# Three of 34 passes of a fused attention kernel written out, and 16 products put before one wait

## The chip, the cores and the metric

The kernel runs on one core of a Trainium2 chip. What counts is the time of one execution on the device in microseconds; of several executions the median is given. The engines are TensorE (PE in the profile, its weight loads PEld), VectorE (DVE), ScalarE (ACT), GpSimd (POOL) and SyncE (SP), which here only starts transfers.

## What is computed

A batch of 64 sequences of 128 rows with 320 channels, with a context of 128 x 192 each, goes through two blocks. All values are float32.

```python
# first block, 8 heads
hs = mha(x @ Wq, enc @ Wk, enc @ Wv)                   # FIRST: enc = the context's first 124 rows
ca_hs1 = mha(ca_q1, x, x)                              # CA: ca_q1 from the context's last 4 rows, "the tokens"
ca_hs2 = mha(ca_hs1 @ Wq, ca @ Wk_ca, ca @ Wv_ca)      # over 4 keys
x = (hs + ca_hs2) @ Wout + b_out + x
# second block, 20 heads
h1 = ln(x); x = attn(h1, h1, q1, k1, v1, o1_w) + x     # SELF
h2 = ln(x); x = attn(h2, context, q2, k2, v2, o2_w) + x  # CROSS
h3 = ln(x); a, g = split(h3 @ ff_w1 + ff_b1)
x = (a * gelu(g)) @ ff_w2 + ff_b2 + x
```

## The kernel before

The batch is cut into 32 steps of two sequences (G = 2, STEPS = 32), and the work on a step into three stages that run in three passes: the first block of step i, the two attentions of the second block of step i - 1, and the feed-forward part (ff) of step i - 2. One pass of the loop does the first stage of one step, the second of the one before and the third of the one before that, so that each engine always has work of another step beside a wait. The loop runs 33 passes, i = 0 to 32, and a tail does the last feed-forward. In pass 0 there is no step for the attentions of the second block nor for ff, in pass 1 none for ff, in pass 32 none for the first block; the loop does those blocks all the same, on zeros or stale tiles, and nothing reads what they give. Before the loop a head loads and scales the weights.

Everything is written out by hand per engine: five instruction streams, each with a loop of its own over i, which meet through semaphores. The list BODY names the results that TensorE puts into its six PSUM banks in turn ("jobs"). `j_next` waits until the bank's last reader is done, and each job ends with an increment of `j_full`, which a reader on ACT (`a_done`) or DVE (`v_done`) waits for. All waits are on counts that grow by a fixed amount per pass (`done`), so each pass must raise each semaphore by the same number.

Names that matter here:

- Heads are taken in units of four. Unit n has the scores (`scores(i, n)`, job S*n*), the row maxima (`maxima`, L1104, on DVE), the maxima turned (`turn_maxima`, L1609, job mx*g*), the scores again with the maximum subtracted (`exponents`, job T*n*), the exponential on ACT (`exps`, L810 and L811), its low part on POOL (`low_probabilities`, L540) and the product with the values (`attend`). Units 0 to 3 are CA, 4 to 13 SELF, 14 to 23 CROSS, 24 to 27 FIRST.
- All matmuls go through `mm` (L1487).
- The query and key tiles of an attention are put together ("stacked") by transfers that SP starts (`spread`, L406): three chunks by three parts for each of Q0T and K0T (tiles Q0s, K0s), K1T (Ks), Q1T and Q2T (Qs). K1T and Q1T (`chunk16`) are split by DVE (`whole_shifted`, L1005) and POOL (`low_split`, L547) first. The cross keys go through DRAM (L394, L398). SP does all in the fixed order of `one_pass`: Q0T, K1T, Q1T, the table M (L439), ten loads of the next step (L384 to L391; `load_next` first waits for DVE's `vca`, the values of the tokens, L1195), K0T 0 and 1, the cross keys, Q2T, K0T 2, K2T, two stores.
- `scores(i, 4)`, the first of SELF, waits for the first chunk of K1T and of Q1T. This wait is called **the S4 wait** below. Ahead of it on TensorE stand the feed-forward jobs ff2 and ff3; behind it S4, S5, T2, vca, S6, S7, V1_0, T3, attends 0 and 1, S8, S9 and mx2.
- DVE takes the extremes of the next step's x (`extremes_x`, L1030, tile xin) for a scale; TensorE turns them (`extremes_turned`, L1716, job mT) and spreads them (mB), and the scale goes over DVE and ACT to POOL.
- The last blocks of a pass are the projections, residuals (L1166) and norms (L1177), with a small power on POOL between (L597, L598). The norm of the first block is what K1T and Q1T of the next pass are made from. DVE's part of Q0T (`low_chunk`, L1011) stands behind that norm in DVE's order.

```python
def one_pass(i, stores):
    put_low(i, "Q0T", 0, Q0s, cQ, Q_PARTS)
    ...
    load_products(i)
    load_next(i)
```

Of the kernel before, what the change touches and what calls it, by code (L numbers as in the profile page):

```python
# [7 lines left out]
B, S, H, C = 64, 128, 320, 192  # L8
# [184 lines left out]
def build(nc, d, out):  # L193
# [4 lines left out]
    with ctx:  # L198
# [182 lines left out]
        def _(sp):  # L381
# [66 lines left out]

            def one_pass(i, stores):
                put_low(i, "Q0T", 0, Q0s, cQ, Q_PARTS)  # L450
                put_low(i, "Q0T", 1, Q0s, cQ, Q_PARTS)
                put_low(i, "Q0T", 2, Q0s, cQ, Q_PARTS)
                put_split(i, "K1T", 0, Ks, cK, K_PARTS)
                put_split(i, "K1T", 1, Ks, cK, K_PARTS)
                put_split(i, "K1T", 2, Ks, cK, K_PARTS)
                put_split(i, "Q1T", 0, Qs, cQ, Q_PARTS)
                put_split(i, "Q1T", 1, Qs, cQ, Q_PARTS)
                put_split(i, "Q1T", 2, Qs, cQ, Q_PARTS)
                load_products(i)
# [12 lines left out]
                put_out(i, 1, stores)  # L472
# [31 lines left out]
        def _(pool):  # L504
# [45 lines left out]
            def x_values(i, b, rest):  # L550
# [4 lines left out]
                scaled = rest[:, b, :].rearrange("p (h e) -> p h e", h=HEADS0)  # L555
                if not isinstance(i, int):
# [79 lines left out]
            nc.gpsimd.memset(whole[:, :, :], 0.0).then_inc(split_done, SPLITS_STEP)  # L636
            with nc.Fori(0, STEPS + 1, engines=[pool.engine], hint_back_edge=True) as i:
                links[0] = 0
# [54 lines left out]
                token_queries(i)  # L693
                assert links[0] == POOL_LINKS
            last_bias(STEPS + 1)

        @block.scalar
        def _(act):
# [115 lines left out]
            def link(i, ins):  # L814

                links[0] += 1
                ins.then_inc(act_done, 1)
                act.wait_ge(act_done, links[0] if isinstance(i, int) else i * ACT_LINKS + ACT_HEAD_LINKS + links[0])

# [58 lines left out]
            assert links[0] == ACT_HEAD_LINKS  # L878
            with nc.Fori(0, STEPS + 1, engines=[act.engine], hint_back_edge=True) as i:
                L = LOOP_JOBS  # L880
# [91 lines left out]
                assert order.next == PER["A"]  # L972
                assert links[0] == ACT_LINKS
            order.restart()
            for t in range(FFT):
# [3 lines left out]
        def _(dve):  # L979
# [372 lines left out]

            with nc.Fori(0, STEPS + 1, engines=[dve.engine], hint_back_edge=True) as i:
                L = LOOP_JOBS
# [119 lines left out]
                assert order.next == PER["V"]  # L1474
                assert links[0] == STEP_LINKS, links[0]
            order.restart()
            for t in range(FFT):
# [5 lines left out]
        def _(pe):  # L1483
# [313 lines left out]

            with nc.Fori(0, STEPS + 1, engines=[pe.engine], hint_back_edge=True) as i:
                L = LOOP_JOBS
# [161 lines left out]
                out_proj(i, 0, 1)  # L1961
                assert filled[0] == PER["J"]
            filled[0] = 0
            for t in range(FFT):
# [75 lines left out]
```

## Time and profile before

| | |
|---|---|
| median of 3 runs | 3696.13 us (3693.54 to 3698.23) |
| the profiled execution | 3700.3 us |
| its span, first to last instruction | 3698.4 us |
| mean granted TensorE clock | 0.956 of full |
| PE busy | 3427.4 us, 93% |
| ACT, DVE, POOL busy | 67%, 61%, 56% |
| first matmul of the loop | 99.36 us |
| start of the tail's feed-forward | 3665.30 us |
| instructions | 114778 |

The page gives the busy time of each engine over the whole span, the same in 40 slices with the granted clock, and the waits by what ended them. Since the program repeats itself, the trace is best read inside one pass (about 108 us), and by comparing passes. PE counts as busy while a matmul is under way, at either clock, so PE's 93% says little about how fast the work goes.

### The profile page before, as it was taken

What the parts mean: (1) busy time and instruction counts of PE and PEld (TensorE: products, weight loads), DVE (VectorE), ACT (ScalarE), POOL (GpSimd) and SP (SyncE); (2) the same over time, 40 slices, a digit from 0 to 9 for tenths busy, and PEclk for the clock granted to TensorE, in tenths of its full rate; (3) what the DMA queues carried; (4) which work ended last, traced back from release to release, by engine and by line L of the source; (5) the groups of instructions that cost most, each with busy time, mean ns of one, the idle gap of its engine ahead of it and who ended that gap; (6) DMA issues with size and microseconds to landing.
All of it is one profiled execution on the core that took longest, in us unless ns stands there. A gap on an engine that the chain in (4) does not pass through costs nothing.

```text
span 3698.4 us, 114778 instructions
## 1 busy us (share of the span) xinstructions
PE 3427.4 (93%) x38842; PEld 2788.6 (75%) x38842; DVE 2269.9 (61%) x5540; ACT 2494.6 (67%) x4428; POOL 2070.6 (56%) x2307
## 2 busy tenths in 40 slices
PE   7899999999999999999999999999999999999999
PEld 7677787777777777777777777787777777777777
DVE  6566666566566656666655666665566666556665
ACT  3576676767767676776767677676767767676774
POOL 1565555556655555655555566555556655555664
PEclk6899999999999999999999999999999999999999
DMA  5211111221111122111112211111221111112111
GB/s 185 56 42 44 40 43 48 50 53 46 47 44 42 45 50 52 46 47 42 43 46 50 52 46 47 42 43 46 50 52 46 47 42 43 45 50 52 46 47 26
DMA packets 316267, 183.06 MB, mean 49 GB/s; under 512 B 50107, under 2 KB 315379, under 8 KB 315507
## 3 DMA queue, kind: packets, MB, share of 16 engines
q1 hardware_dynamic: 303936, 173.93, 18.5%
q8 instruction: 367, 6.01, 0.7%
q10 hardware_dynamic: 11955, 3.04, 0.4%
q14 instruction: 9, 0.07, 0.0%
HBM read 70.59 MB, written 24.67 MB: 26 GB/s over the span
## 4 chain that ended last, share of the span: by engine, by line
PE 44%; issue 20%; POOL 11%; DVE 7%; SPq 6%; ACT 5%; DMA 5%; POOLq 1%; ACTq 1%; DVEq 0%
PE bank L1487 41%; SPq L406 5%; DMA Qs<-cQ 5%; DVE mx L1104 4%; PE bank L1514 2%; ACT PT L811 2%; POOL rstd L598 2%; POOL cK L547 1%; POOL cQ L547 1%; ACT L794 1%; POOL c L592 1%; ACT P L810 1%; POOL X L517 1%; POOL rstd L597 1%; PE bank L1609 1%
## 5 line engine op out<-in xcount | busy, mean ns | idle before, releaser
L540 POOL TENSOR_TENSOR PT<-P,PT 128x512 f16<-128x512 f32 (+1 forms) x924 | 1066.9, 1156 | 808.5 <-ACT PT L811 806.2
L1487 PE MATMUL bank<-hT,w_ff_w 128*128 128x256 f16 x5440 | 644.0, 273 | 29.3 <-DVE G L1018 29.3
L1104 DVE TENSOR_REDUCE mx<-bank 128x4 f32<-128x512 f32 (+1 forms) x924 | 588.5, 682 | 115.7 <-PE bank L1487 108.3
L1487 PEld LDWEIGHTS bank<-hT,w_ff_w 128*128 128x128 f16 x5440 | 518.3, 98 | 100.5 <-DVE G L1018 41.0
L1487 PE MATMUL bank<-mxs,pick 84*128 84x128 f16 (+1 forms) x3696 | 513.6, 223 | 0.0
L1183 DVE SCALAR_TENSOR_TENSOR F<-bank,ff_b,gate 128x256 f32<-128x256 f32 x340 | 160.0, 481 | 435.9 <-ACT gate L794 435.9
L1487 PE MATMUL bank<-w_ff,F 128*128 128x320 f32 x1360 | 418.4, 443 | 1.3 <-DVE F L1183 1.3
L1487 PEld LDWEIGHTS bank<-mxs,pick 84*128 84x128 f16 (+1 forms) x3696 | 380.6, 105 | 4.0
L1487 PE MATMUL bank<-Ks,Qs 96*128 96x128 f16 x2640 | 236.0, 235 | 148.3 <-DMA Qs<-cQ 144.3
L1487 PEld LDWEIGHTS bank<-V,PT 128*128 128x128 f16 (+1 forms) x9504 | 336.2, 96 | 48.7 <-issue 23.5
L1487 PE MATMUL bank<-Qs,Ks 96*128 96x128 f16 x2640 | 359.3, 219 | 11.2 <-DVE mxs L1113 7.3
L1487 PE MATMUL bank<-V,PT 128*128 128x17 f16 (+1 forms) x9504 | 352.2, 172 | 0.0
L1487 PEld LDWEIGHTS bank<-Ks,Qs 96*128 96x128 f16 x2640 | 175.4, 105 | 219.3 <-issue 188.1
L794 ACT ACTIVATE gate<-bank,ff_b,scale 128x256 f32<-128x256 f32 x340 | 184.0, 562 | 211.1 <-PE bank L1487 172.7
L810 ACT ACTIVATE P<-bank,log_p,held 128x512 f32<-128x512 f32 x330 | 253.6, 768 | 78.8 <-PE bank L1487 44.4
L597 POOL TENSOR_TENSOR rstd<-mv,eps 128x1 f32<-128x1 f32 x198 | 44.7, 226 | 467.5 <-DVE mv L1171 467.5
L1487 PEld LDWEIGHTS bank<-w_ff,F 128*128 128x128 f32 x1360 | 239.9, 190 | 78.9 <-issue 6.5
L1487 PEld LDWEIGHTS bank<-Qs,Ks 96*128 96x128 f16 x2640 | 252.1, 98 | 30.3 <-DVE mxs L1113 22.7
L810 ACT ACTIVATE P<-bank,log_p,exp_self 128x512 f32<-128x512 f32 x330 | 254.8, 772 | 19.6 <-POOL PT L540 9.8
L811 ACT ACTIVATE PT<-bank,log_p,exp_self 128x512 f16<-128x512 f32 x330 | 253.8, 769 | 0.0
L811 ACT ACTIVATE PT<-bank,log_p,held 128x512 f16<-128x512 f32 x330 | 252.3, 765 | 0.0
L1005 DVE TENSOR_SCALAR whole<-bank,q_factor,qk_b 128x256 f32<-128x256 f32 (+1 forms) x297 | 157.4, 539 | 124.8 <-ACT cQ L723 89.7
(290 smaller groups left out, 7310.6 us busy)
## 6 DMA issues: line engine op xcount, KB each, us to landing
Qs<-cQ SPq DMA_DIRECT2D x402, 64.0 KB, 2.6
Ks<-scratch_k SPq DMA_DIRECT2D x99, 160.0 KB, 4.6
Ks<-cK SPq DMA_DIRECT2D x198, 64.0 KB, 2.6
Q0s<-cQ SPq DMA_DIRECT2D x198, 60.0 KB
K0s<-cK SPq DMA_DIRECT2D x198, 60.0 KB
xin<-in_x SPq DMA_DIRECT2D x34, 320.0 KB, 3.5
out<-X SPq DMA_DIRECT2D x64, 160.0 KB, 1.8
xT<-in_xT SPq DMA_DIRECT2D x68, 128.0 KB, 2.1
```

Of the source, the lines that this page charges most:

```text
L406: sp.dma_start(dst[y * e:(y + 1) * e, at:at + heads, :], src[0:rows[k], part, k, :])\
L540: nc.gpsimd.tensor_tensor(PT[0:keys, n % PT_SLOTS, 1, :], P[0:keys, n % P_SLOTS, :], PT[0:keys, n % PT_SLOTS, 0, :], ALU.subtract).then_in ...
L547: nc.gpsimd.tensor_tensor(dst[0:r, 1, k, :], whole[0:r, m % 3, :], dst[0:r, 0, k, :], ALU.subtract)\
L597: link(i, nc.gpsimd.tensor_tensor(rstd[:, j, b:b + 1], mv[:, j, b, 1:2], eps[:, :], ALU.add))
L598: nc.gpsimd.tensor_tensor(rstd[:, j, b:b + 1], rstd[:, j, b:b + 1], minus_half[:, :], ALU.pow)\
L794: nc.scalar.activation(gate[:, t % 2, :], bank[:, 0:GS], ACT.Gelu, scale=scale[:, 1:2], bias=ff_b[:, FFT + t:FFT + t + 1]).then_inc(a_done, 1)
L810: nc.scalar.activation(P[0:keys, n % P_SLOTS, :], bank[0:keys, :], ACT.Exp, bias=log_p[0:keys, :], scale=by)
L811: nc.scalar.activation(PT[0:keys, n % PT_SLOTS, 0, :], bank[0:keys, :], ACT.Exp, bias=log_p[0:keys, :], scale=by).then_inc(a_done, 1)
L1005: nc.vector.tensor_scalar(whole[0:r, m % 3, :], bank[0:r, 0:GS], q_factor[0:r, :], qk_b[0:r, c + k:c + k + 1], ALU.mult, ALU.add).then_inc ...
L1104: nc.vector.tensor_reduce(mx[:, g % 2, 4 * u:4 * u + 4], bank[:, :].rearrange("p (h s) -> p h s", h=4)[:, :, 0:keys], axis=AX.X, op=ALU.ma ...
L1183: nc.vector.scalar_tensor_tensor(out=F[:, t, :], in0=bank[:, GS:2 * GS], scalar=ff_b[:, t:t + 1], in1=gate[:, t % 2, :], op0=ALU.add, op1= ...
L1487: return nc.tensor.matmul(o, lhsT, rhs, start=start, stop=stop)
```

## The change

There are two parts.

**Written out.** Passes 0, 1 and 32 leave the loop, on all five engines, and are written out in straight code without the blocks that have no step: pass 0 without SELF, CROSS and ff; pass 1 without ff; pass 32 without CA, FIRST and what they need. The loop runs i = 2 to 31. Where blocks are left out, a `left_out` raises the semaphores by what they would have: on ACT, DVE and POOL by a drain with an increment, on TensorE by one product of 1 x 1 for each semaphore, behind the wait for the bank of the next job. On SP passes 0 and 1 were written out already; of the transfers only the table M and the ten loads of pass 32 go, the other transfers of passes 0, 1 and 32 stay, those of blocks without a step too.

**16 products.** In `scores`, `j_next` moves ahead of the waits for the stacked tiles, and at S4 16 matmuls of 128 x 128 weights by 512 columns (f16, from the ff weights) go into S4's bank between the two. S4 writes over them; nothing reads them. They stand in passes 1 to 32.

```diff
@@ -94,6 +94,7 @@
 SPLITS_STEP = 9
 LOADS_STEP = 16 * 10
 STACK_LOADS = 16 * 3
+KEEP_BUSY = 16
...
-            def one_pass(i, stores):
+            def one_pass(i, stores, last=False):
...
-                load_products(i)
-                load_next(i)
+                if not last:
+                    load_products(i)
+                    load_next(i)
...
-            with sp.Fori(2, STEPS + 1) as i:
+            with sp.Fori(2, STEPS) as i:
                 one_pass(i, True)
+            one_pass(STEPS, True, True)
+            for landed in stacked["K0T"]:
+                sp.wait_ge(landed, (STEPS + 1) * 48)
...
+            def left_out(i, split_done_by=0, low_p_by=0, pool_done_by=0, rstd_ready_by=0, xc_ready_by=0, c16_ready_by=0, xa_ready_by=0, vx_ready_by=0, x16_ready_by=0, ca_ready_by=0):
+
+                if split_done_by:
+                    pool.drain().then_inc(split_done, split_done_by)
+                if low_p_by:
+                    pool.drain().then_inc(low_p, low_p_by)
...
-            with nc.Fori(0, STEPS + 1, engines=[act.engine], hint_back_edge=True) as i:
+            def left_out(i, a_done_by=0, c_scaled_by=0, c_high_by=0, act_done_by=0, next_ready_by=0, x_scaled_by=0, x_high_by=0, exp4_ready_by=0, factor_ready_by=0):
+
+                if a_done_by:
+                    act.drain().then_inc(a_done, a_done_by)
...
-                elif b == 0 and att != CA:
+                bank = j_next(i, LOOP_JOBS, f"S{n}")
+                if (att, b, u) == (SELF, 0, 0):
+
+                    for _ in range(KEEP_BUSY):
+                        mm(bank[:, 0:2 * GS], w16["ff_w1"][:, 0, 0, 0:128], w16["ff_w1"][:, 0, 0, 0:2 * GS])
+                if b == 0 and att != CA:
...
-                bank = j_next(i, LOOP_JOBS, f"S{n}")
...
-            with nc.Fori(0, STEPS + 1, engines=[pe.engine], hint_back_edge=True) as i:
+            def left_out(i, j_full_by=0, pv_done_by=0):
+
+                n = min(filled[0], PER["J"] - 1)
+                bank_free(i, LOOP_JOBS, n)
+                o = j_bank[n % J_BANKS][0:1, 0:1]
+                if pv_done_by:
+                    mm(o, one_row[:, 0:1], one_row[:, 0:1]).then_inc(pv_done, pv_done_by)
+                if j_full_by:
+                    mm(o, one_row[:, 0:1], one_row[:, 0:1]).then_inc(j_full, j_full_by)
+                filled[0] += j_full_by
+
+            i = 0
+            L = LOOP_JOBS
+            filled[0] = 0
+            left_out(i, j_full_by=1)
+            chunk(i, "Q0T", 0, "Wq", x16, PASSES_X, AT0, CH0)
+            chunk(i, "Q0T", 1, "Wq", x16, PASSES_X, AT0, CH0)
+            left_out(i, j_full_by=1)
+            chunk(i, "Q0T", 2, "Wq", x16, PASSES_X, AT0, CH0)
...
+            extremes_turned(i, L)
+            left_out(i, pv_done_by=2, j_full_by=5)
+            extremes_everywhere(i, L, 2)
+            left_out(i, pv_done_by=6, j_full_by=6)
+            chunk(i, "K0T", 1, "Wk", c16, PASSES_C, AT0, CH0)
+            left_out(i, j_full_by=3)
+            scores4(i)
+            left_out(i, j_full_by=6)
+            chunk(i, "K0T", 2, "Wk", c16, PASSES_C, AT0, CH0)
+            left_out(i, j_full_by=6)
+            values(i, "V0", 1, "Wv")
+            chunk(i, "K2T", 0, "k2", c16, PASSES_C, AT1, CH1)
+            left_out(i, j_full_by=7)
...
+            with nc.Fori(2, STEPS, engines=[pe.engine], hint_back_edge=True) as i:
...
```

On TensorE, at the S4 wait in the loop (L1494 and L2233 are `done`, the number for a wait on a bank; L1595 and L2339 the wait for the stacked tiles), before:

```order
L1494 REGISTER_ALU
L1487 MATMUL bank<-hT,w_ff_w 128x256 x16
L1494 REGISTER_ALU
L1487 MATMUL bank<-hT,w_ff_w 128x256 x16
L1595 ISA
L1494 REGISTER_ALU
L1487 MATMUL bank<-Ks,Qs 128x128 x4
```

and now:

```order
L2233 REGISTER_ALU
L2226 MATMUL bank<-hT,w_ff_w 128x256 x16
L2233 REGISTER_ALU
L2226 MATMUL bank<-w_ff_w 128x512 x16
L2339 ISA
L2226 MATMUL bank<-Ks,Qs 128x128 x4
```

Between ff3 and S4 the number for the bank comes before the wait for the transfers, and the 16 products stand between them.

On TensorE, in pass 0, from the turned extremes (ident,ext_wide; mT) over mB (diag,ones_square) and the chunks 1 and 2 of K0T (c,w_Wk) with s4 (M,whole) between, as it is now:

```order
L2459 MATMUL bank<-ident,ext_wide 128x128
L2226 MATMUL bank<-one_row 1x1 x2
L2226 MATMUL bank<-diag,ones_square 128x2
L2226 MATMUL bank<-one_row 1x1 x2
L2226 MATMUL bank<-c,w_Wk 120x256 x5
L2226 MATMUL bank<-one_row 1x1
L2226 MATMUL bank<-M,whole 128x32 x6
L2226 MATMUL bank<-one_row 1x1
L2226 MATMUL bank<-c,w_Wk 80x256 x5
```

Before, the last of these stood behind this much more (from K0T's chunk 1 to chunk 2):

```order
L1487 MATMUL bank<-c,w_Wk 120x256 x5
L1494 REGISTER_ALU
L1487 MATMUL bank<-w_o_w,hTn 128x320 x8
L1494 REGISTER_ALU
L1518 REGISTER_ALU
L1487 MATMUL bank<-w_o_w,hTn 128x320 x8
L1494 REGISTER_ALU
L1487 MATMUL bank<-hT,w_ff_w 128x256 x16
L1494 REGISTER_ALU
L1565 ISA
L1487 MATMUL bank<-M,whole 128x32 x6
L1674 ISA
```

Between the chunks of K0T the projections of SELF and the feed-forward jobs are gone, and a 1 x 1 product stands for them.

## Rows read from the trace of the kernel before

**Rows 1.** Waits of the whole span: who waited, for whom, us in total, times, longest.
```profile
PE bank L1487 <- DMA Qs<-cQ: 144.3, 49, 5.0
...
SPq L444 <- DVE vca L1195: 62.4, 31, 2.4
```

**Rows 2.** Stretches of pass 13, its start and around S4: length, PE, PEld, DVE, ACT, POOL busy, granted clock.
```profile
1508.00:1514.00 6.00, 5.24 (x48) 4.71 (x47) 4.33 (x12) 3.11 (x7) 3.00 (x6) 1.00 0.02 5
1528.50:1533.00 4.50, 0.00 (x0) 0.00 (x0) 0.94 (x2) 1.28 (x3) 3.86 (x5) 0.97 0.30 78
1533.00:1539.50 6.50, 6.35 (x34) 4.00 (x35) 3.06 (x5) 2.73 (x3) 1.15 (x1) 0.50 0.17 46
```

**Rows 3.** Timeline of pass 13: start, us, engine, line, what [idle before, ended by].
```profile
1524.79 3.66 PE L1487 MATMUL bank<-hT,w_ff_w 128*128 128x256 f16 x32
...
1533.15 1.03 PE L1487 MATMUL bank<-Ks,Qs 96*128 96x128 f16 x8 [4.71 <-DMA Qs<-cQ]
...
1537.40 0.48 DVE L1195 TENSOR_TENSOR vca<-bank,maskv 64x320 f32<-64x320 f32 x1 [2.32 <-PE bank L1487]
...
1541.88 0.28 PE L1609 MATMUL bank<-ident,mx 128*20 128x128 f32 x1 [0.26 <-DVE mx L1104]
...
1547.49 0.82 DVE L1030 TENSOR_REDUCE ext_wide<-xin 128x1 f32<-128x640 f32 x1 [0.24 <-DMA xin<-in_x]
```

**Rows 4.** Timeline of pass 5, with the S4 of pass 6.
```profile
671.41 0.62 PE L1487 MATMUL bank<-Ks,Qs 96*128 96x128 f16 x8 [3.92 <-DMA Qs<-cQ]
...
674.70 0.48 DVE L1195 TENSOR_TENSOR vca<-bank,maskv 64x320 f32<-64x320 f32 x1 [1.57 <-PE bank L1487]
...
678.75 0.28 PE L1609 MATMUL bank<-ident,mx 128*20 128x128 f32 x1 [0.26 <-DVE mx L1104]
...
684.32 0.82 DVE L1030 TENSOR_REDUCE ext_wide<-xin 128x1 f32<-128x640 f32 x1 [0.19 <-DMA xin<-in_x]
...
777.30 0.39 PE L1487 MATMUL bank<-Ks,Qs 96*128 96x128 f16 x4 [4.02 <-DMA Qs<-cQ]
```

**Rows 5.** A stretch of pass 5, columns as in rows 2.
```profile
672.40:676.90 4.50, 4.50 (x24) 2.50 (x23) 2.50 (x5) 2.73 (x3) 1.15 (x1) 0.62 0.16 44
```

**Rows 6.** Timeline of pass 14: mx2, and extremes that waited for no transfer.
```profile
1650.11 0.28 PE L1609 MATMUL bank<-ident,mx 128*20 128x128 f32 x1 [0.26 <-DVE mx L1104]
...
1655.40 0.81 DVE L1030 TENSOR_REDUCE ext_wide<-xin 128x1 f32<-128x640 f32 x1
```

**Rows 7.** Timeline of SP's queue, pass 0 and the start of pass 1.
```profile
113.96 7.35 SPq L406 DMA_DIRECT2D Q0s<-cQ  x9
...
127.89 6.41 SPq L406 DMA_DIRECT2D Qs<-cQ  x9
...
142.09 0.45 SPq L391 DMA_DIRECT2D xin<-in_x  x1
...
166.66 1.75 SPq L398 DMA_DIRECT2D Ks<-scratch_k  x3
173.61 5.75 SPq L406 DMA_DIRECT2D Qs<-cQ  x9
179.40 2.45 SPq L406 DMA_DIRECT2D K0s<-cK  x3
...
221.79 7.20 SPq L406 DMA_DIRECT2D Q0s<-cQ  x9
```

**Rows 8.** The page, part 6: a transfer, how often, KB each, us from issue to landing.
```profile
xin<-in_x SPq DMA_DIRECT2D x34, 320.0 KB, 3.5
```

**Rows 9.** Timeline of pass 0: TensorE.
```profile
132.77 0.62 PE L1487 MATMUL bank<-Ks,Qs 96*128 96x128 f16 x8 [2.19 <-DMA Qs<-cQ]
...
178.13 2.37 PE L1487 MATMUL bank<-w_ff,F 128*128 128x320 f32 x8
```

**Rows 10.** Timeline of pass 0: the first exponential of CROSS, the last of the pass.
```profile
184.86 0.78 ACT L810 ACTIVATE P<-bank,log_p,held 128x512 f32<-128x512 f32 x1 [1.34 <-PE bank L1487]
...
206.83 0.80 ACT L811 ACTIVATE PT<-bank,log_p,factor 124x512 f16<-124x512 f32 x1
```

More of the change, by code:

```diff
@@ L638, in _ @@
+            token_queries(i)
+            assert links[0] == POOL_LINKS
+            with nc.Fori(2, STEPS, engines=[pool.engine], hint_back_edge=True) as i:
                 links[0] = 0
@@ new lines, in _ @@
+            high_tokens(i, L)
+            turn_factors(i, done(i, PER["V"] - 1, "V"))
+            assert order.next == PER["A"]
+            assert links[0] == ACT_LINKS
+            i = 1
+            L = LOOP_JOBS
+            order.restart()
+            links[0] = 0
+            left_out(i, a_done_by=1)
+            high_chunk(i, "Q0T", 0, cQ, CH0[0], FQ0)
+            high_chunk(i, "Q0T", 1, cQ, CH0[1], FQ0)
+            high_blocks(i, "XT0_0", hTn, 0)
+            high_chunk(i, "Q0T", 2, cQ, CH0[2], FQ0)
@@ new lines, in _ @@
+            high_out(i, 2, 1)
+            exps(i, 26)
+            exps(i, 27)
+            high_out(i, 0, 0)
+            first_part(i, "V2", 1, V2, HEADS1, D1, fixed[:, F2:F2 + 1])
+            high_out(i, 0, 1)
+            high_blocks(i, "XT2_0", hT3, 0)
+            high_blocks(i, "XT2_1", hT3, 1)
+            high_tokens(i, L)
+            turn_factors(i, done(i, PER["V"] - 1, "V"))
+            assert order.next == PER["A"]
+            assert links[0] == ACT_LINKS
+            with nc.Fori(2, STEPS, engines=[act.engine], hint_back_edge=True) as i:
@@ new lines, in _ @@
+            i = 0
+            L = LOOP_JOBS
+            links[0] = 0
+            order.restart()
+            left_out(i, v_done_by=1)
+            low_chunk(i, "Q0T", 0, cQ, CH0[0], FQ0)
+            low_chunk(i, "Q0T", 1, cQ, CH0[1], FQ0)
+            left_out(i, v_done_by=1)
+            low_chunk(i, "Q0T", 2, cQ, CH0[2], FQ0)
+            left_out(i, v_done_by=4)
+            maxima(i, 0)
+            maxima(i, 1)
+            left_out(i, v_done_by=2)
+            maxima(i, 2)
+            maxima(i, 3)
@@ new lines, in _ @@
+            normalise(i, 7)
+            left_out(i, xh_ready_by=1)
+            whole_heads(i, 1)
+            left_out(i, xh_ready_by=1)
+            low_part(i, "V2", 1, V2, HEADS1, D1, fixed[:, F2:F2 + 1])
+            residual(i, 0, 0)
+            low_out(i, 0, 1)
+            left_out(i, v_done_by=2)
+            low_tokens(i, L)
+            residual(i, 0, 1)
+            norm(i, 0, 0)
+            norm(i, 0, 1)
+            assert order.next == PER["V"]
+            assert links[0] == STEP_LINKS, links[0]
@@ new lines, in _ @@
+            low_maxima(i, 3)
+            copy_hT(i, "caT0", 0, CH0)
+            copy_hT(i, "caT1", 1, CH0)
+            diagonal(i, L, 2)
+            normalise(i, 2)
+            step_sizes(i, L)
+            left_out(i, v_done_by=1)
+            low_out(i, 1, 0)
+            normalise(i, 3)
+            left_out(i, v_done_by=3)
+            low_out(i, 1, 1)
+            low_chunk(i, "K0T", 1, cK, CH0[1], FK0)
+            residual(i, 1, 0)
+            residual(i, 1, 1)
+            norm(i, 1, 0)
@@ new lines, in _ @@
+            norm(i, 1, 1)
+            left_out(i, v_done_by=1)
+            scores4(i)
+            low_blocks(i, "XT1_0", hTn, 0)
+            low_blocks(i, "XT1_1", hTn, 1)
+            left_out(i, v_done_by=1)
+            whole_shifted(i, "Q2T", 0, 6)
+            whole_shifted(i, "Q2T", 1, 6)
+            whole_shifted(i, "Q2T", 2, 6)
+            low_chunk(i, "K0T", 2, cK, CH0[2], FK0)
+            maxima(i, 14)
+            maxima(i, 15)
+            left_out(i, v_done_by=1)
+            maxima(i, 16)
@@ L1354, in _ @@
+            assert order.next == PER["V"]
+            assert links[0] == STEP_LINKS, links[0]
+            with nc.Fori(2, STEPS, engines=[dve.engine], hint_back_edge=True) as i:
                 L = LOOP_JOBS
@@ new lines, in _ @@
+            residual(i, 2, 0)
+            left_out(i, v_done_by=1)
+            residual(i, 2, 1)
+            left_out(i, v_done_by=1, dve_done_by=1, o_done_by=1)
+            norm(i, 2, 0)
+            left_out(i, v_done_by=1)
+            norm(i, 2, 1)
+            left_out(i, v_done_by=3, dve_done_by=1, var_ready_by=1)
+            low_blocks(i, "XT2_0", hT3, 0)
+            low_blocks(i, "XT2_1", hT3, 1)
+            left_out(i, v_done_by=2, dve_done_by=1, var_ready_by=1, xh_ready_by=2)
+            assert order.next == PER["V"]
```

1000 lines of the change are left out of this document (994 added, 6 removed).

## The prediction, written before the changed kernel ran

> **What bounds the kernel now.** I read the waits first, then one pass in stretches and as a timeline, then the passes against each other. The list of waits has TensorE standing still for the transfers of the stacked queries: 144.3 us in 49 times [rows 1]. The long ones are one per pass, at S4, so at most 144.3 / 33 = 4.4 us each. The stretches show what follows: TensorE does nothing for some 4.5 us, at full clock nearly to the end, and the next 6.5 us run at a granted clock of 0.50, the lower of its two levels, 1.2 instead of 2.4 GHz, while it is busy throughout [rows 2]. So the wait costs twice: once as idle time, and once more in the products behind it.
>
> The timeline gives the size. From S4 to mx2, the first thing that waits for the row maxima of SELF, pass 13 takes 1541.88 - 1533.15 = 8.7 us [rows 3]. In pass 5 the clock came back sooner (0.62 over 4.5 us) and the same stretch took 7.3 us [rows 4, 5]. The next S4 then came 105.9 us after this one [rows 4], where the mean of the 31 distances from pass 1 on is 107.8. Three more passes with 7.35 us to mx2 are followed by 106.3, 106.8 and 106.8 us. The trace thus holds the experiment already: what is gained in this stretch is gained in the pass.
>
> What hangs on it is DVE's order. The extremes of xin begin 5.3 us behind mx2 where their transfer is there (1655.40 - 1650.11) [rows 6], otherwise when it lands. Over the 30 passes 2 to 31 they begin on average 14.4 us behind S4 (14.3 in pass 13, 12.9 in pass 5) [rows 3, 4], and from them to the next pass all passes take the same within 0.1 us. I therefore price the change at this point.
>
> **The 16 products.** *Their own cost.* 32 products of 256 columns take 3.66 us to the end of the last, so 0.109 us each [rows 3]; 512 columns twice that, 16 make 3.5 us. They begin when ff3 is issued and S4's bank was read long before, so they lie inside the wait of at most 4.4 us on average, which stays: it ends when transfers land that SP issues back to back from Q0T on (27 of them in 20.3 us in pass 0, 113.96 to 134.30) [rows 7]. Without that cover they would cost their 3.5 us in every pass. Behind TensorE in this time stands nothing but S4.
>
> *The clock.* About 0.9 us of idle time is left, 0.2 to 1.5 over the passes. The trace has two neighbours: 6.00 - 5.24 = 0.8 us without work at the start of each pass leave the clock at 1.00 [rows 2]; idle of 2.2 us before S4 of pass 0 was followed by the low clock [rows 9]. 0.9 is nearer the first, and I take it that the clock stays up in passes 2 to 31.
>
> *What that is worth.* At full clock the stretch is S4 and S5 0.45, T2 0.55, vca 1.2 (4 float32 products at (2.37 - 0.43) / 7 = 0.28, and a gap) [rows 9], S6 and S7 0.45, V1_0 1.1 (8 x 320 columns at 0.136), T3 0.47, attend 0.3, and S8 to mx2 1.2: together 5.7 us, against 8.7. DVE would then ask for xin at 5.7 + 5.3 = 11.0. It isn't there: SP loads it only after vca, which DVE finishes 4.7 us behind S4 in pass 13 and 3.8 in pass 5 [rows 3, 4]. xin could be read 9.6 and 9.1 us after that; with vca done at 2.8 it lands at 11.9 to 12.8, since SP's present wait for vca, 62.4 / 31 = 2.0 us [rows 1], is just used up. I take 12.4. So the extremes move from 14.4 to 12.4, 2.0 us per pass, and the transfer of xin is what comes late next. Over the 30 passes in the loop: **60 us**. Bounds: as good as pass 5 only, 14.4 - 12.9 = 1.5, makes 45; if xin never held, 14.4 - 11.0 = 3.4, makes 102. The page on "TensorE: Matmul & The Clock Gate" of the Trainium skill, in its section on the back-to-back issue gap, gives about 131 ns per product of 512 columns for a sustained stream of load and product; by it, an estimate, the 16 would take 2.1 us and leave 2.2 us idle. No row here has 512 columns in this type; those of 256 scale to 218 ns, and what it would mean if the page were right is a rival below.
>
> In passes 1 and 32 I count nothing for the products: ff2 and ff3, or CA's jobs, no longer stand before the wait, it grows to some 7 to 9 us, and what is left beyond 3.5 is longer than the 2.2 that was enough in pass 0.
>
> **Written out, pass 0.** Of TensorE's work most goes, but the path becomes SP's queue and the chain of four units. Q0T's transfers start at 113.96 as before; they and those of K1T and Q1T are still made, to 134.3 [rows 7]. The loads, which waited for vca, start at once, 2.5 us sooner, xin is issued at 139.6 rather than 142.09 and lands 3.5 us later [rows 7, 8], at 143.1. Two reductions, mT, mB and K0T 1 through ACT and DVE: an estimate of 6 us from the single durations, 149. Then, each by its row: K0T 1 2.45, cross keys 1.75, Q2T 5.75, K0T 2 2.45, at 161.4, and 2.0 to land: 163.4 for FIRST's second unit, where it is 179.40 + 2.45 + 2.0 = 183.9 now [rows 7]. From there to Q0T of pass 1 it is 37.9 us now, with CROSS's ten units between; then it is maxima 4.5, four exponentials of 1.35 and copies 6.7, the last low part 1.2, and the tail of products, residual and norm, for which I take 10 (now 221.79 - 207.63 = 14.2, in a queue with others) [rows 7, 10]: 22.4, so 185.8. **36 us** saved; bounds 28 (twice the tail's slack, and products at the low clock) and 42.
>
> **Pass 1.** It lacks ff: 160 products of 256 columns at 0.109 and 40 in float32 at 0.28, 28 us of TensorE. Up to S4 it was cover for SP's transfers, and gives nothing. Between S4 and the end of SELF ACT's exponentials set the pace. Behind them the gelus and products go out of a serial chain, about 3 us, and two feed-forward pieces before mx4 2 more; from 184.86 on ACT works without a break to 207.63 [rows 10] and is not shortened. **5 us**; bounds 0 and 15.
>
> **Pass 32.** No CA, FIRST or chunks: mx2 needs 5 instead of 8.9 us at the low clock (no T2, vca, T3, attends), some 4; two copies before mx4 1; the last exponentials and the first block's tail leave the end, where the tail's ff waits only for CROSS's norm, 6; one less job at the start 1. **12 us**; bounds 6 and 20.
>
> Drains, 1 x 1 products and longer programs: at most some 0.1 us each on engines that have idle time; they count as nothing as long as the semaphores they raise are not the last ones, and make 5 us at worst in three passes. The loop's exit shows no gap in front of the tail, so I add none.
>
> **The sum.** 60 + 36 + 5 + 12 = 113 us. Against the profiled execution's 3700.3 us (span 3698.4) that is 3587; it lies 4.2 above the median of 3696.13, so the median becomes **3583 us**.
>
> **The rivals.**
> - *The clock still falls.* The rest of the wait, or the mix of work behind it, is enough to lower it. For it: the 2.2 us of pass 0 [rows 9]. Against it: only 0.9 us are left. Only the 53 us of the written-out passes remain: 3643. Chance 0.10. The page's shorter products would lead here too: products in half their time leave 2.2 us, as in pass 0, and the time is the same 3643 us, worked out from the same rows; chance 0.05.
> - *xin does not hold.* The transfer lands sooner than I think, or DVE's delay isn't on TensorE's path, whose jobs behind mT then run on: up to 102 + 53 = 155, 3541. Chance 0.12.
> - *Less from the passes written out.* The chain of four units runs at the low clock and the left-out jobs make waits of their own; half of 53: 3610. Chance 0.08.
> - *Slower.* The products themselves run at 1.2 GHz: 7.0 us, 2.6 beyond the wait, 32 times 83, less 53: 3726. It decides from the point where they end 53 / 32 = 1.7 us behind the landing. Against it: the clock is at 1.00 when the wait begins, and stays for most of it [rows 2]. Chance 0.02.
>
> My forecast has 0.63. **The range**, 3540 to 3620, takes in the forecast with its bounds, the free xin and the smaller gain of the passes, and leaves out the fallen clock and the slower case, 0.17. Below 0.2%, 7.4 us, a measurement of this kernel can't tell from no change; only a cancelling of gain and longer wait would fall there, 0.01. Faster 0.97, slower 0.02.
>
> **What the changed profile would show.** The 16 products right behind ff3, 3.5 us; a wait of about 0.9 us; granted clock 1.00 over passes 2 to 31, mean about 0.99; mx2 5.7 us behind S4; the extremes at about 12.4 with some 1.3 us of wait for xin in every pass; a distance of 105.8 us between S4s; S4 of pass 1 near 204; the tail's ff at 3552. A clock of 0.5 behind S4 in the loop, or extremes that wait for nothing, would show the second term wrong; an S4 of pass 1 beyond 212 the third.

## The result, and the profile after

| | before | changed |
|---|---|---|
| median | 3696.97 us | 3739.02 us |
| range of the runs | 3693.54 to 3698.23 | 3731.01 to 3757.15 |
| profiled execution, its span | 3700.3, 3698.4 | 3757.15, 3755.2 |
| mean granted clock | 0.956 | 0.939 |

The ratio is 1.0124, with a 95% interval of 1.0091 to 1.0157: the changed kernel is **slower by 1.2%**. The forecast was 3583 us, 3.1% faster. The profiled execution of the changed kernel was its slowest of four, 18 us over the median; its shares below add up to its own 3755.2, so they are somewhat larger than those of a middling execution.

I split both traces at S4 of passes 1, 2 and 32 (239.60, 347.41 and 3580.56 before; 206.73, 317.94 and 3632.07 now):

| stretch | before | now | difference | forecast |
|---|---|---|---|---|
| start to S4 of pass 1 | 239.6 | 206.7 | -32.9 | -36 |
| pass 1 | 107.8 | 111.2 | +3.4 | -5 |
| passes 2 to 31, each | 107.77 | 110.47 | +2.7 | -2.0 |
| pass 32 and tail | 117.8 | 123.1 | +5.3 | -12 |

The loop carries the result: 30 x 2.7 = 81 us in this execution. The list of waits of the changed kernel, the whole span, TensorE's and DVE's part (who waited, for whom, us in total, times, longest):

```profile
PE bank L2459 <- DVE V L1443: 65.6, 31, 3.3
PE bank L2226 <- DMA Qs<-cQ: 36.8, 56, 3.0
PE bank L2226 <- issue: 26.0, 10, 3.4
...
DVE ext_wide L1449 <- DMA xin<-in_x: 78.2, 33, 8.7
```

The 144.3 us of [rows 1] have become 36.8. In their place stands a wait at mT (L2459), once per pass, at most 3.3 us: mT's bank and its operand come from DVE, and DVE waits 78.2 us for xin. The main rows of one pass, pass 10, as the timelines of TensorE, DVE and SP's queue have it:

```profile
1191.87 3.62 PE L2226 MATMUL bank<-w_ff_w 128*128 128x512 f16 x16
1196.17 0.61 PE L2226 MATMUL bank<-Ks,Qs 96*128 96x128 f16 x8 [0.68 <-DMA Qs<-cQ]
1201.88 0.28 PE L2352 MATMUL bank<-ident,mx 128*20 128x128 f32 x1 [0.26 <-DVE mx L1523]
1205.63 0.40 SPq L392 DMA_DIRECT2D xin<-in_x  x1
1209.20 0.82 DVE L1449 TENSOR_REDUCE ext_wide<-xin 128x1 f32<-128x640 f32 x1 [1.95 <-DMA xin<-in_x]
1211.14 0.32 PE L2459 MATMUL bank<-ident,ext_wide 128*128 128x128 f32 x1 [1.90 <-DVE V L1443]
1242.75 0.62 PE L2226 MATMUL bank<-Ks,Qs 96*128 96x128 f16 x8
```

Up to mx2 this is the forecast to the tenth: 16 products in 3.6 us, 0.7 us of wait left, mx2 5.71 us behind S4 (8.7 in [rows 3]). Then TensorE stands 1.9 us at mT, and from mT to S14 (the last row) it takes 31.6 us; before it was 28.7 on average. The stretches of the same pass say why (columns as in rows 2: length, the five engines, granted clock, and then the DMA engines' share and GB/s):

```profile
1191.50:1196.00 4.50, 3.99 (x21) 1.78 (x19) 0.94 (x2) 1.88 (x3) 4.46 (x6) 1.00 0.31 80
1196.00:1202.00 6.00, 5.58 (x78) 4.27 (x79) 4.33 (x8) 4.13 (x6) 1.16 (x1) 1.00 0.26 67
1209.00:1212.00 3.00, 1.10 (x25) 0.93 (x23) 2.74 (x7) 2.03 (x4) 2.19 (x3) 1.00 0.08 21
1212.00:1220.00 8.00, 8.00 (x94) 7.00 (x91) 1.83 (x8) 4.34 (x6) 3.72 (x4) 0.57 0.01 2
```

The clock is 1.00 behind S4, where it was 0.50, and 0.57 behind mT, where it was 1.00. **The low clock has moved with the wait.** It follows mT in 27 of the 30 passes of the loop. In 8 of the 30 there is a second stop at the end of the pass, before ff0, the first products of the next one, and nothing in the profile ends it. The timeline of TensorE at the start of pass 16, and the stretch behind it, where the clock is down too (0.61):

```profile
1832.61 2.44 PE L2226 MATMUL bank<-hT,w_ff_w 128*128 128x256 f16 x16 [2.63 <-issue]
```

```profile
1833.00:1837.00 4.00, 4.00 (x25) 3.66 (x24) 0.72 (x1) 1.84 (x3) 3.77 (x5) 0.61 0.00 0
```

So theory A: the forecast holds up to mx2, the wait for xin becomes idle time of TensorE, and this idle time costs the clock. Its rival, B: it is the written-out code that slows the loop.

### The profile page after: what moved, and what is told of

Same layout as the page of the kernel before. It is cut to its first block, busy times and chain, and to the rows that moved or that the text cites. A ratio compares the mean times of both kernels' runs of the same rounds, so it can differ in the third digit from the quotient of the medians.

```text
span 3755.2 us, 111650 instructions
## 1 busy us (share of the span) xinstructions
PE 3464.1 (92%) x38162; PEld 2789.7 (74%) x38162; DVE 2197.6 (59%) x5366; ACT 2419.3 (64%) x4281; POOL 2012.4 (54%) x2242
## 3 DMA queue, kind: packets, MB, share of 16 engines
q8 instruction: 353, 5.78, 0.6%
## 4 chain that ended last, share of the span: by engine, by line
PE 46%; issue 15%; SPq 9%; DVE 8%; POOL 8%; DMA 7%; ACT 5%; POOLq 1%; ACTq 1%; DVEq 1%
PE bank L2226 43%; SPq L407 5%; DMA Qs<-cQ 4%; DVE mx L1523 3%; DMA xin<-in_x 3%; PE bank L2253 2%; SPq L386 1%; POOL cQ L552 1%; ACT PT L977 1%; ACT P L976 1%; SPq L385 1%; POOL rstd L603 1%; DVE V L1443 1%; POOL cK L552 1%; ACT L960 1%
## 5 line engine op out<-in xcount | busy, mean ns | idle before, releaser
L545 POOL TENSOR_TENSOR PT<-P,PT 128x512 f16<-128x512 f32 (+1 forms) x896 | 1034.0, 1156 | 879.1 <-ACT PT L977 864.6
L1523 DVE TENSOR_REDUCE mx<-bank 128x4 f32<-128x512 f32 (+1 forms) x896 | 571.1, 681 | 107.2 <-PE bank L2226 101.9
L2226 PE MATMUL bank<-mxs,pick 84*128 84x128 f16 (+1 forms) x3584 | 535.3, 233 | 0.0
L2226 PE MATMUL bank<-Qs,Ks 96*128 96x128 f16 x2560 | 393.6, 237 | 20.0 <-DVE mxs L1532 14.4
L2226 PE MATMUL bank<-w_ff,F 128*128 128x320 f32 x1280 | 396.3, 445 | 1.3 <-DVE F L1602 1.3
L960 ACT ACTIVATE gate<-bank,ff_b,scale 128x256 f32<-128x256 f32 x320 | 173.6, 563 | 206.1 <-PE bank L2226 171.1
L2226 PEld LDWEIGHTS bank<-Qs,Ks 96*128 96x128 f16 x2560 | 267.4, 107 | 38.6 <-DVE mxs L1532 29.1
L2226 PEld LDWEIGHTS bank<-w_ff,F 128*128 128x128 f32 x1280 | 227.2, 191 | 75.4 <-issue 7.7
L2226 PE MATMUL bank<-Ks,Qs 96*128 96x128 f16 x2560 | 209.8, 221 | 48.0 <-DMA Qs<-cQ 36.8
L2226 PEld LDWEIGHTS bank<-Ks,Qs 96*128 96x128 f16 x2560 | 158.0, 98 | 105.6 <-issue 37.7
```

The costliest lines, as they stand in the source:

```text
L545: nc.gpsimd.tensor_tensor(PT[0:keys, n % PT_SLOTS, 1, :], P[0:keys, n % P_SLOTS, :], PT[0:keys, n % PT_SLOTS, 0, :], ALU.subtract).then_in ...
L960: nc.scalar.activation(gate[:, t % 2, :], bank[:, 0:GS], ACT.Gelu, scale=scale[:, 1:2], bias=ff_b[:, FFT + t:FFT + t + 1]).then_inc(a_done, 1)
L1523: nc.vector.tensor_reduce(mx[:, g % 2, 4 * u:4 * u + 4], bank[:, :].rearrange("p (h s) -> p h s", h=4)[:, :, 0:keys], axis=AX.X, op=ALU.ma ...
L2226: return nc.tensor.matmul(o, lhsT, rhs, start=start, stop=stop)
```

## The experiments

### Each part alone

The first kernel is the one before with only this edit in `scores`; the second is the changed kernel without the products.

```diff
+                bank = j_next(i, LOOP_JOBS, f"S{n}")
+                if (att, b, u) == (SELF, 0, 0):
+                    for _ in range(KEEP_BUSY):
+                        mm(bank[:, 0:2 * GS], w16["ff_w1"][:, 0, 0, 0:128], w16["ff_w1"][:, 0, 0, 0:2 * GS])
```

> The kernel before, all 33 passes in the loop, with only the 16 products. Theory A (the wait has moved: SELF is quicker up to mx2, then mT stands 2.2 us for xin and the clock falls there): a distance of 110 to 110.5 us between S4s as in the changed kernel, so some 33 x 2.5 = 80 us more than before, 3765 to 3785; clock 0.5 from about 15 to 25 us behind S4. Theory B (the longer, written-out code slows the loop, for instance by late instructions at its start, and the products do what was forecast): 106 us per pass, 3635 to 3645.

Measured: 3666.72 us (3652.36 to 3673.12), ratio 0.9934 (0.9912 to 0.9957). Faster, where theory A as stated wanted 80 us slower; yet 22 us above B's range.

```diff
-KEEP_BUSY = 16
+KEEP_BUSY = 0
```

> The changed kernel without its 16 products (the bank's wait still ahead of the transfers' wait). Theory A: the loop's passes as before, 107.8; pass 0 33 us shorter, passes 1 and 32 no shorter or some 3 to 5 us longer each because TensorE has less to do there and its clock falls: 3668 to 3675. Theory B (written-out code slows the loop): passes of 109 or more, 3700 and above. The forecast of record had 53 us from these passes: 3643.

Measured: 3678.54 us (ten runs, 3672.40 to 3695.16), ratio 0.9962 (0.9946 to 0.9978), with loop passes of 108.1 us. A little above A. In its profiled execution S4 of pass 1 stands at 210.0, 29.6 us sooner than before, but pass 1 takes 111.9 us (107.8 before) and pass 32 with the tail 121.1 (117.8 before). Each part alone gains, 26 and 14 us beside 3692.81 for before, and together they lose 42. The trace of the products alone explains half of it. Two of its passes in the timeline, S4, the extremes and mT of each, and then the stretches of 10 us behind mT:

```profile
1202.25 0.61 PE L1488 MATMUL bank<-Ks,Qs 96*128 96x128 f16 x8 [0.74 <-DMA Qs<-cQ]
1214.87 0.82 DVE L1031 TENSOR_REDUCE ext_wide<-xin 128x1 f32<-128x640 f32 x1 [1.53 <-DMA xin<-in_x]
1216.81 0.32 PE L1721 MATMUL bank<-ident,ext_wide 128*128 128x128 f32 x1 [1.49 <-DVE V L1025]
...
2470.17 0.61 PE L1488 MATMUL bank<-Ks,Qs 96*128 96x128 f16 x8 [0.64 <-DMA Qs<-cQ]
2482.82 0.82 DVE L1031 TENSOR_REDUCE ext_wide<-xin 128x1 f32<-128x640 f32 x1 [1.58 <-DMA xin<-in_x]
2484.77 0.32 PE L1721 MATMUL bank<-ident,ext_wide 128*128 128x128 f32 x1 [1.53 <-DVE V L1025]
```

```profile
1217.00:1227.00 10.00, 10.00 (x170) 9.44 (x170) 2.47 (x10) 8.53 (x13) 6.96 (x7) 1.00 0.01 3
2485.00:2495.00 10.00, 10.00 (x131) 8.87 (x130) 2.45 (x10) 5.66 (x9) 4.61 (x4) 0.66 0.02 3
```

With almost the same wait at mT the clock held once and fell once. Here it fell in 8 of 30 passes; these take 109.2 us, the 22 others 105.3, half a microsecond under the forecast's 105.8. (This was its fastest execution, 14 us under the median, and that of the changed kernel its slowest, so 8 against 27 is likely to be on the wide side.) The extremes stand 12.3 us behind S4 (forecast 12.4) and wait 1.25 us for xin (forecast 1.3). For the products alone the forecast was right in all but the clock behind mT.

In the changed kernel xin is issued at the same place (9.3 us behind S4 in both), but the page has it landing 3.9 us later instead of 3.0, the wait is 2.2 us, and nearly every pass falls. The row of the changed kernel, then that of the products alone:

```profile
xin<-in_x SPq DMA_DIRECT2D x33, 320.0 KB, 3.9
```

```profile
xin<-in_x SPq DMA_DIRECT2D x34, 320.0 KB, 3.0
```

What holds up a transfer by 0.9 us?

### A transfer of instructions in xin's flight

The DMA view of the changed kernel, pass 10, 8.5 to 12.5 us behind S4, lists a packet that isn't the kernel's:

```profile
q1 hardware_dynamic: 1033, 0.81, 72.3%
q8 instruction: 1, 0.02, 1.6%
```

Its 1.6% of 16 engines over 4 us are 1.0 us of one engine. In the 17 us behind S4, instruction packets stand at 3 to 4 and 10 to 11 us in all 30 loop passes of the changed kernel, and at 7 to 8 and 15 to 16 us with the products alone. The page counts 353 of them with 5.78 MB, so 16 KB each:

```profile
q8 instruction: 353, 5.78, 0.6%
```

Between two of them TensorE works off some 120 products with as many weight loads, so they are its program, at about 64 bytes an instruction (16 KB over some 250; an estimate). The loop's products are the same in both kernels, but in the changed one the loop stands behind two passes of straight code. Theory C: the place of the loop within 16 KB decides when the packets are fetched, and in the changed kernel one is fetched while xin flies. The test moves this place and leaves the loop as it is: 32 products of 1 x 1 in float32, each two matmuls with two weight loads, so 128 instructions or 8 KB, once before the loop.

```diff
+PAD = 32
                 pe.wait_ge(diag_ready, i + 2)
+                if isinstance(i, int) and i < 0:
+                    for _ in range(PAD):
+                        mm(bank[0:1, 0:1], ones_square[:, 0:1], diag[:, 0:1])
```

> The changed kernel with 32 products of 1 x 1 (float32) put once before the loop on TensorE, 8 KB of its program, half of the 16 KB that one instruction transfer carries. Theory C (an instruction transfer of TensorE falls into the flight of xin in every pass, at S4 + 10, and holds it up 1 us; with the wait for xin at 2.2 instead of 1.3 us the clock falls in nearly every pass): the instruction transfers move to about S4 + 6.5 and S4 + 15, xin lands 3.0 us after its issue instead of 3.9, the clock falls in a third of the passes, and the time comes to 3640 to 3660. Rival (the position in the program does not matter; the wait for xin is that long because of what else the change moved): same as the changed kernel, 3725 to 3755.

Measured: **3636.31 us** (3635.98 to 3644.65), ratio 0.9855 (0.9835 to 0.9875), 4 us under the expected range. 103 us for 8 KB of code that runs once. The DMA view, 8.5 to 12.5 us behind S4 of pass 11, has no line for instructions any more, and in the one of the whole span xin lands in 3.0 us:

```profile
q1 hardware_dynamic: 942, 0.67, 61.1%
```

```profile
xin<-in_x SPq DMA_DIRECT2D x33, 320.0 KB, 3.0
```

The packets stand at 7 to 8 and 15 to 16 us, the clock falls in 7 of 30 passes, and no pass stops at ff0. The same edit on the products alone:

> The products alone (3667 us unshifted), with the same 8 KB put before the loop. Theory C: here the shift does harm; the instruction transfer at S4 + 15 comes to about S4 + 11, into the flight of xin, xin lands up to 1 us later, the clock falls behind mT in most passes, 109 to 110 us per pass: 3740 to 3780. Rival: no difference, 3655 to 3675.

Measured: 3758.32 us (three executions, 3737.99 to 3760.00), ratio 1.0161 (1.0127 to 1.0195), as theory C had it. 8 KB turn the gain of the products into a loss. The profiled execution took 3804.89, 1.8% more than the fastest, and is left out of these figures. It shows the packets at 3 to 4 and 10 to 11 us. Its wait for xin of 2.1 us, its 23 of 30 passes with the clock down behind mT and its 19 with ff0 held up can't be set beside the other kernels' counts. A whole packet, 64 products, on the changed kernel:

```diff
-PAD = 32
+PAD = 64
```

> The changed kernel with 64 products of 1 x 1 before the loop, 16 KB of program, a whole instruction transfer. Theory C (only the place within 16 KB matters): the instruction transfers stand at S4 + 3 and S4 + 10 again, and the time is that of the changed kernel, 3725 to 3760. Rival (it was the added work before the loop that helped, not the shift): 3630 to 3660 as with 8 KB.

Measured: 3780.95 us (3740.43 to 3794.62), ratio 1.0248 (1.0220 to 1.0275). The gain of the half is gone, so it was the place and not the added work. But the time isn't that of the changed kernel, as expected (3725 to 3760): it is higher even against its own 3693 for before, its runs spread over 54 us, and I leave open why. In its profiled execution, the fastest, the packets stand at 3 to 4 and 10 to 12 us again, and 23 of 30 passes fall behind mT.

In ten of the fourteen kernels xin is the last of the ten loads. In four of them (before, changed, whole packet, and the one with products at mT, below) a packet starts 1.0 to 1.6 us behind the issue of xin on average, and xin lands 3.7 to 4.2 us after that issue; the execution left out above shows the same. In the five others no packet stands there, or only 2.7 us behind the issue, and it lands in 3.0 to 3.1 us. So the kernel before had such a packet too (3.5 us in [rows 8], the median), with little wait behind it.

The kernel before with the shift alone:

> The kernel before with the 8 KB shift alone. Theory C: xin was not what the extremes waited for there (0.3 us), and the clock falls at S4 in any case: 3683 to 3700, within 0.2% of before. Rival (the loop is quicker at this place for another reason, and the changed kernel owed its gain after the shift to that): under 3670.

Measured: 3728.44 us (3708.10 to 3736.77), ratio 1.0101 (1.0083 to 1.0118). **A miss**, 28 us above the range: I had looked only at xin. The waits of TensorE have a new line (first), and one of its ten stops is this in the timeline:

```profile
PE bank L1488 <- issue: 28.0, 10, 3.0
```

```profile
536.68 1.92 PE L1488 MATMUL bank<-hT,w_ff_w 128*128 128x256 f16 x16 [3.01 <-issue]
```

The stops explain the slower time only in part, as far as is known: the profiled execution was the fastest (3708.10), its span is 8 us longer than before's with 28.0 us of stops in it, and its passes without a stop take 107.3 us instead of 107.8. What makes the median 35 us longer isn't in this trace.

In five kernels (changed, before shifted, products alone shifted, whole packet, and xin first, below) instruction packets stand 3 us ahead of ff0 and at ff0; these stop there in 8, 10, 19, 6 and 17 of 30 passes (the 19 in the execution that is left out above). In the nine others ff0 never stops, and there is one packet, at most 1 us ahead of it in nearly every pass. The kernels with 12 products more and 16 fewer in the loop, from the same start as the changed one, are among these nine, so the loop's length counts as well as its place. I infer that TensorE then reaches the loop's head before its instructions do, and that the stop of 2.6 us in the changed kernel is this; the profile itself names nothing that ends it. Why it comes in some passes only is open.

### Taking the wait at mT away

Two remedies. Products before mT, as at S4 (12, in `extremes_turned`, between the wait for the bank and the one for the extremes):

```diff
                 bank = j_next(i, jobs, "mT")
+                if not isinstance(i, int) or i >= 1:
+                    for _ in range(KEEP_BUSY_MT):
+                        mm(bank[:, 0:2 * GS], w16["ff_w1"][:, 0, 0, 0:128], w16["ff_w1"][:, 0, 0, 0:2 * GS])
                 pe.wait_ge(ext_ready, i + 2)
```

> The changed kernel with 12 further unread products ahead of the wait for the extremes at mT (passes 1 to 31), 12 x 0.226 = 2.7 us for a wait of 1.6 to 3.3. Theory A: the wait for xin stays, filled; the clock stays at 1.00 behind it, S14 about 44.2 us behind S4, 106 to 106.5 us per pass: 3739 - 30 x 4.2 = 3605 to 3620. Rival (it is not the idle time that lowers the clock there): clock still 0.5 behind mT and 110 us or more per pass, 3735 or above.

Measured: 3720.94 us (3719.68 to 3721.52), ratio 1.0076 (1.0056 to 1.0096). Neither. The timeline shows my error:

```profile
1210.85 0.82 DVE L1450 TENSOR_REDUCE ext_wide<-xin 128x1 f32<-128x640 f32 x1 [1.92 <-DMA xin<-in_x]
1212.72 2.76 PE L2227 MATMUL bank<-w_ff_w 128*128 128x512 f16 x12 [1.79 <-DVE V L1444]
1215.32 0.27 PE L2463 MATMUL bank<-ident,ext_wide 128*128 128x128 f32 x1
```

The last reader of mT's bank is V, which DVE does behind the extremes. So the products begin when the wait is over, and cost their 2.7 us. It still beats the changed kernel by 18 us, for two reasons that this run doesn't separate: ff0 never stops, and the clock falls in 9 of 30 passes, not 27. This although TensorE stands idle in front of the 12 products for 2.1 us on average (0.5 to 2.8), as it did in front of mT. So the length of the idle time alone doesn't decide the fall; what follows it counts too, as far as this one run shows.

And xin first of the ten loads, ahead of the wait for vca, which it doesn't need. All ten raise one semaphore, and the extremes wait for the full count, so this takes the largest load off the end of the ten; what they wait for afterwards is the last of the other nine (`carep`, 48 KB):

```diff
+                sp.wait_ge(xa_ready, i * G + G)
+                sp.wait_ge(vx_ready, i * G + G)
+                load_xin(i + 1)
                 sp.wait_ge(v_done, v_job(i, LOOP_JOBS, "vca"))
                 sp.wait_ge(c16_ready, i + 1)
-                sp.wait_ge(xa_ready, i * G + G)
                 sp.wait_ge(ca_ready, i + 1)
-                sp.wait_ge(vx_ready, i * G + G)
```

> The changed kernel with the load of xin issued first of the ten and ahead of the wait for vca. Theory A: the last transfer of the ten lands about 2 us sooner, mT waits under 1 us, the clock does not fall behind it, S14 42.5 us behind S4 and 104.5 to 105.5 us per pass, as in the one pass of the changed kernel where mT waited 0.4 us: 3739 - 30 x 5 = 3580 to 3600. Rival (the clock falls at whatever wait comes next, or it is worn out by the 16 products themselves): a fall at another place of the pass, over 108 us per pass, above 3670.

Measured: 3632.76 us (3629.81 to 3670.20), ratio 0.9832 (0.9812 to 0.9852). Above the expected 3580 to 3600. The extremes wait 0.7 us, 8 of 30 passes fall behind mT, and 17 stop at ff0; those with neither take 104.5 us, as theory A had it. (The profiled execution was the slowest, 37 us over the median, so these counts are likely to be on the high side.) What was missing was the place:

> The changed kernel with xin loaded first (median 3633 unshifted), with the same 8 KB. Theory C: the last of the ten transfers is no longer held up at S4 + 10 and lands in 2 instead of 3 us; mT waits 0.5 us at most; 103.6 to 104.5 us in passes without a fall: 3585 to 3615. Rival: no difference, 3625 to 3670.

Measured: **3579.56 us** (3577.33 to 3580.21), ratio 0.9692 (0.9676 to 0.9708), 5 us under the expected range. The extremes wait 0.4 us for the loads; one fall in 30 passes, no stop at ff0, 104.7 us per pass.

### The passes written out

Passes 1 and 32 back in the loop, pass 0 still written out, xin first, and 39 products so that the loop stands a whole number of 16 KB behind the place in the kernel with the products alone:

```diff
-            with nc.Fori(2, STEPS, engines=[pe.engine], hint_back_edge=True) as i:
+            with nc.Fori(1, STEPS + 1, engines=[pe.engine], hint_back_edge=True) as i:
```

> Only pass 0 written out, passes 1 to 32 in the loop with all blocks, 16 products, xin first, and 39 products of 1 x 1 before the loop so that the loop's program stands at the same place within 16 KB as in the kernel with the products alone. Theory A and C: pass 0 keeps its 29 us, passes 1 and 32 with ff and the first block in them keep the clock up and are no longer than a loop pass; 104 to 104.5 us per pass: S4 of pass 1 at 206, S4 of pass 32 near 3435, end near 3555 to 3580. Rival (passes 1 and 32 written out did gain, as the forecast had it): longer by their 17 us than that, and S4 of pass 2 later than 315.

Measured: **3568.35 us** (3567.22 to 3570.28), ratio 0.9665 (0.9649 to 0.9682), the best of all, at a mean clock of 0.98. Pass 1 in this kernel, and without ff in the one before it (S4 to S4 each):

```profile
211.00:315.00 104.00, 100.60 (x1175) 81.26 (x1173) 65.84 (x162) 74.41 (x132) 61.86 (x69) 1.00 0.18 45
```

```profile
210.00:319.00 109.00, 92.24 (x1063) 72.94 (x1062) 63.72 (x154) 68.29 (x123) 62.77 (x70) 0.84 0.18 43
```

With some 110 more products pass 1 is 4.5 us shorter (104.4 against 108.9), with the clock at 1.00 and not 0.84. Pass 32 with the tail takes 114.2 against 118.8 us, at 1.00 and not 0.88. The clock is what I take for the cause. The two kernels also differ in that one has these passes in the loop and the other in straight code, and no run separates this from the work left out.

The same with xin loaded last:

> Pass 0 written out and 16 products, the loop's program at the good place, but xin still loaded last. Theory A and C: mT waits 1.3 us, the clock falls behind it in a third of the passes at 4 us each and the wait itself costs 0.9 more than with xin first: 32 x (0.9 + 1.3) = 70 us over 3568, so 3625 to 3645, and 25 to 35 under the kernel with the products alone (3667) for pass 0. Rival (pass 0 and the products do not add up): outside of that.

Measured: 3632.69 us (3629.42 to 3649.80), ratio 0.9832 (0.9816 to 0.9848). As expected. The profiled execution, its slowest, falls behind mT in 14 of 30 passes, 109.1 us each against 105.4. Its median is 34 us under that of the products alone, which have the loop at the same place and pass 0 in it (3666.72). In the two traces S4 of pass 1 comes 22 us sooner (213.7 against 236.1), so not all of the 34 is seen in pass 0. xin first is worth 64 us (3632.69 less 3568.35).

### How much idle time the clock bears

Half the products in the best kernel:

```diff
-KEEP_BUSY = 16
+KEEP_BUSY = 8
```

> The last kernel (pass 0 written out, xin first, 3568 us) with 8 instead of 16 products at S4: they last 1.8 us and leave some 2.3 of the wait. Theory A (idle time of this length before S4 lets the clock fall): 0.5 behind S4 in most passes, mx2 8 to 8.9 us behind S4, 107 us per pass, 3640 to 3670. Rival (the clock bears 2.3 us here, the 16 are more than is needed): mx2 at 5.7, 3560 to 3580.

Measured: 3604.00 us (3599.25 to 3607.11), ratio 0.9753 (0.9737 to 0.9769), between the two. Two passes with the same wait in the timeline, S4 and mx2 of each, and then the stretches of 7 us behind S4:

```profile
2431.41 0.61 PE L1730 MATMUL bank<-Ks,Qs 96*128 96x128 f16 x8 [1.97 <-DMA Qs<-cQ]
2437.12 0.28 PE L1856 MATMUL bank<-ident,mx 128*20 128x128 f32 x1 [0.26 <-DVE mx L1247]
...
2535.50 0.72 PE L1730 MATMUL bank<-Ks,Qs 96*128 96x128 f16 x8 [1.94 <-DMA Qs<-cQ]
2544.42 0.28 PE L1856 MATMUL bank<-ident,mx 128*20 128x128 f32 x1 [0.26 <-DVE mx L1247]
```

```profile
2431.50:2438.50 7.00, 6.67 (x91) 5.09 (x91) 5.32 (x10) 5.05 (x8) 1.99 (x3) 1.00 0.42 120
2535.50:2542.50 7.00, 7.00 (x38) 4.30 (x39) 3.06 (x5) 2.73 (x3) 1.41 (x2) 0.53 0.38 109
```

The clock fell in 17 of 32 passes, after waits of 1.75 to 3.1 us, and held after waits of up to 2.7. So about 2 us is a toss-up here, and the 16 products are worth 36 us more than 8.

## Why the prediction was wrong

**Right.** The products: 3.6 us (3.5 predicted), inside the wait, clock 1.00 behind S4, mx2 at 5.71 (5.7). The transfer of xin as what comes late next: extremes at 12.3, wait 1.25, passes of 105.3 us with the products alone where the clock held (12.4, 1.3 and 105.8). Pass 0: -32.9 for 36, inside the bounds of 28 and 42; in the nine other kernels with pass 0 written out S4 of pass 1 stands at 205.7 to 213.7, so 26 to 34 us sooner than before. The products took 226 ns each, about what the rows of 256 columns scaled to (218). The trace disagrees here with the 131 ns that the Trainium skill gives in "TensorE: Matmul & The Clock Gate", section on the back-to-back issue gap.

**The step that failed** is in the second term: "So the extremes move from 14.4 to 12.4, 2.0 us per pass, and the transfer of xin is what comes late next." I priced the new wait as idle time alone. In the loop of the changed kernel the extremes came at 13.3 us, TensorE stood 2.2 us at mT, the low clock followed in 27 of 30 passes, and a pass took 110.5 us, not 105.8. The first paragraph of the prediction had just said that a wait costs twice, and [rows 9] had a wait of 2.2 us with the low clock behind it; I held that row against the rest of the old wait and not against the new one. With the products alone a pass with a fall behind mT takes 109.2 - 105.3 = 3.9 us more, of which 0.4 is its longer wait; that is twice the gain of 2.0.

**The second error** is a cost put at nothing: "Drains, 1 x 1 products and longer programs ... count as nothing". As engine time they are. But the written-out code moves the loop to another place in TensorE's program. There an instruction packet flies with xin (3.9 us to land, 3.0 without one), and others stand at the loop's head. That goes with 27 falls in 30 passes and 8 stops at ff0; after the shift the same loop has 7 and none. The shift of 8 KB is worth 3739 - 3636 = 103 us, nearly as much as my whole sum of 113. No row that I had read showed it; the page of before counts the instruction packets, and I had not asked where in a pass they stand. The 3.5 us that xin took to land there [rows 8] already had one in it.

**The third** is the sign of passes 1 and 32: -5 and -12 forecast, +3.4 and +5.3 measured. The work left out was, as I read it, what kept the clock up: in pass 1 TensorE is busy 95.3 of 111 us at a clock of 0.82, where it was 100.1 of 107 at 0.96. I had costed only what the blocks take, at the clock that they had beside them.

Of the rivals none was right. The one for slower had the products overrun the wait, which they did in a third of the passes by tenths of a microsecond, at full clock. What none of them had was the same mechanism at the next wait. Without the bad place the changed kernel is at 3636, still 53 us above the forecast: that part is the falls that remain and passes 1 and 32.

**Slips in the working** that decided nothing: from the extremes to the next pass's S4 the 30 passes take 92.9 to 94.0 us, not the same within 0.1; the landing "at 11.9 to 12.8" comes from 2.8 + 9.1 and 2.8 + 9.6 and so ends at 12.4; 4.4 - 2.1 is 2.3, not 2.2.

## What to carry to other kernels

When a wait of TensorE is filled or removed, look where it stands next and price that wait with the clock behind it, too; fill or remove both, or count on losing the gain. Leaving work out of a pass can lengthen it when that work kept TensorE's clock up. And in a loop of several instruction packets per pass, as here, an edit that moves the loop in its program can shift when instructions are fetched: before judging a change of a per cent, measure it at two places of the loop, half a packet (8 KB here) apart.

## What the hardware showed unexpectedly

- 8 KB of code run once before a loop changed the time by -103 us (3739 to 3636), +92 (3667 to 3758), +35 (3693 to 3728) and -53 (3633 to 3580), and with it where the 16 KB instruction packets fall in the pass. 16 KB gave no gain. In the third kernel the trace accounts for the time only in part.
- A 320 KB load, the last of ten, took 3.9 us instead of 3.0 with one such packet in its flight, and the packet itself takes 1.0 us of an engine. That the packet holds it up is inferred from the places of both in nine kernels; on which of the 16 DMA engines it went isn't in these views. With xin as the first of the ten loads a packet stood 1.0 us behind its issue in every loop pass too, and it landed in 3.0 us all the same; so the packet in its flight isn't enough by itself.
- Idle time of TensorE of 1.1 to 2.7 us was followed by the low clock in some passes and not in others, with waits equal to 0.05 us. With 12 products right behind it, 2.1 us of idle time on average was followed by a fall in 9 of 30 passes; without them, 2.2 us in 27 of 30.
